# Weights by hardware queues with casts on chip, and a constant row summed earlier, in an eight-core attention kernel

## The reference

```
xn  = layernorm(x)                          # over the 1024 features
Q,K,V = xn@W1+b1, xn@W2+b2, xn@W3+b3        # each 1024 x 1024
attn  = softmax(Q K^T / 32)                 # 4096 x 4096 for each batch
out1  = (attn V) @ W4 + b4
W_real, W_imag = unfold(G1_R,G2_R), unfold(G1_I,G2_I)   # 512 x 512 each
out2  = [xr@Wr^T - xi@Wi^T + br,  xr@Wi^T + xi@Wr^T + bi] # complex linear layer on xn's halves
result = x + out1 + out2
```

## Time and profile before

| | us |
|---|---|
| median of 3 runs | 1297.14 |
| range of the runs | 1293.47 to 1345.95 |
| the profiled execution | 1296.3 |
| its span on the slowest core (core 6) | 1294.7 |
| spans of the 8 cores | 1287.4 to 1294.7 |
| PE busy | 1276.1 (99% of the span) |
| DVE, ACT, POOL busy | 522.5, 329.4, 169.5 |

### The profile page before, as it was taken

How to read it: one execution, slowest core, us unless ns; L and a number is a source line. 1 busy time by engine, 2 the same in 40 slices (tenths; PEclk the granted TensorE clock), 3 DMA queues, 4 the chain that set the end, 5 groups by cost and what they waited for, 6 DMA issues and landing times.

```text
span 1294.7 us, 16471 instructions; the slowest of 8 cores (1287.4 to 1294.7 us)
## 1 busy us (share of the span) xinstructions
PE 1276.1 (99%) x6142; PEld 588.7 (45%) x6142; DVE 522.5 (40%) x860; ACT 329.4 (25%) x463; POOL 169.5 (13%) x123
## 2 busy tenths in 40 slices
PE   6999998999999999999999999999999999999998
PEld 3555443444444444444444444444444444444444
DVE  4455661444144424442344333333433244414442
ACT  2453332312321122222112321122222212221111
POOL 2232132111011111111111111111111011101110
PEclk8999999999999999999999999999999999999999
DMA  9879294122222213321223223220233122322222
GB/s 134 202 188 203 49 196 73 33 66 66 65 65 65 66 33 82 76 71 33 66 65 79 52 52 79 66 66 33 65 79 80 39 65 66 65 65 66 65 66 66
DMA packets 178846, 100.74 MB, mean 78 GB/s; under 512 B 160824, under 2 KB 162896, under 8 KB 178768
## 3 DMA queue, kind: packets, MB, share of 16 engines
q1 hardware_dynamic: 173152, 91.28, 29.5%
q0 software_dynamic: 5408, 8.39, 4.4%
q10 hardware_dynamic: 208, 0.02, 0.0%
HBM read 51.43 MB, written 16.78 MB: 53 GB/s over the span
## 4 chain that ended last, share of the span: by engine, by line
PE 97%; DMA 2%; issue 0%; DVE 0%; POOL 0%; SPq 0%; ACT 0%; POOLq 0%; DVEq 0%; ACTq 0%
PE ring L788 34%; PE po L830 33%; PE ring L672 8%; PE pf L652 4%; PE po L652 4%; PE pf L815 2%; PE pf L801 2%; PE pf L808 2%; PE po L709 1%; PE ring L639 1%; PE pf L760 1%; PE po L760 1%; PE pf L709 1%; DMA V<-W 1%; DMA GT<-bim 1%; PE po L861 1%
## 5 line engine op out<-in xcount | busy, mean ns | idle before, releaser
L788 PE MATMUL ring<-XT,GT 128*128 128x512 bf16 x2048 | 447.4, 379 | 0.2 <-ACT Et L611 0.2
L830 PE MATMUL po<-V,ET 128*128 128x512 bf16 x1984 | 438.3, 379 | 0.0
L788 PEld LDWEIGHTS ring<-XT,GT 128*128 128x128 bf16 x2048 | 200.3, 98 | 242.0 <-issue 0.6
L830 PEld LDWEIGHTS po<-V,ET 128*128 128x128 bf16 x1984 | 194.1, 98 | 234.1
L475 DVE TENSOR_REDUCE mx<-ring 128x1 f32<-128x512 f32 x256 | 176.8, 691 | 210.8 <-PE ring L788 210.6
L501 DVE SCALAR_TENSOR_TENSOR xr<-po,rrv,xr 128x1024 f32<-128x1024 f32 x31 | 39.8, 1284 | 419.8 <-PE po L830 419.8
L326 POOL TENSOR_TENSOR xr<-xr,cb 128x1024 f32<-128x1024 f32 x32 | 75.0, 2343 | 939.6 <-DVE junk L480 939.6
L606 ACT ACTIVATE S<-ring 128x512 f32<-128x512 f32 x128 | 76.4, 597 | 423.7 <-DVE mx L475 423.6
L611 ACT ACTIVATE Et<-ring,ngm 128x2048 bf16<-128x2048 f32 x32 | 63.0, 1968 | 300.4 <-DVE ngm L494 300.4
L672 PE MATMUL ring<-XT,A 128*128 128x512 bf16 x512 | 113.7, 383 | 3.3 <-ACT GT L550 3.3
L672 PEld LDWEIGHTS ring<-XT,A 128*128 128x128 bf16 x512 | 50.4, 99 | 65.2 <-issue 5.9
(11 more groups left out here) (104 smaller groups left out, 641.8 us busy)
## 6 DMA issues: line engine op xcount, KB each, us to landing
xr<-x SPq DMA_DIRECT2D x40, 512.0 KB, 3.3
out<-xr SPq DMA_DIRECT2D x31, 512.0 KB, 2.6
S<-x SPq DMA_DIRECT2D x16, 512.0 KB, 6.1
Et<-x SPq DMA_DIRECT2D x8, 512.0 KB, 5.8
V<-W POOLq DMA_DIRECT2D x2, 1024.0 KB, 16.6
V<-W POOLq DMA_DIRECT2D x8, 256.0 KB, 18.4
V<-W POOLq DMA_DIRECT2D x4, 512.0 KB, 20.0
A<-W POOLq DMA_DIRECT2D x4, 512.0 KB, 8.9
```

Source lines behind the costliest of these rows:

```text
L788: mm = e.matmul(bank[tb % 4], GT[:, c, rows(i % 4)], XT[:, c, tb * 512:(tb + 1) * 512], start=(c == 0), stop=(c == 7))
L830: mm = e.matmul(po[:, v * 512:(v + 1) * 512], ET[:, i % 2, tj, :], V[:, tj, v * 512:(v + 1) * 512], start=(tj == 16), stop=(tj == 15))
```

## The change

- W4's left half no longer comes by one casting load of POOL. ACT issues four plain fp32 loads (pairs of row blocks p = 0 to 3) into a part of XT that is still unused (`W4stage`); DVE casts pairs 0 and 2, ACT pairs 1 and 3.
- W3's row 0 comes as fp32 by SP's first load (`W3stage`) and is cast by DVE. SP's small loads stand behind it, ACT's small loads have moved to SP.
- PE turns W3's row 0 before the G1 transposes, and row 1 inside fold piece 0, whose matmuls wait pair by pair.
- b4 is loaded on SP behind tile 18, the FFN biases behind tile 27, both into `xr[:, 1, :]`; DVE sums them behind tiles 24 and 28. ACT's `evict_g(0)` waits for the last weight operation (`s_wdv` 28) instead of the sums.
- PE's waits for the transposes of tiles 30 and 31 move from `g_group(0)` to the last block of the first scores.

The core of the diff:

```diff
-    bias_in = GT[:, 0:4, :].rearrange("p a n -> p (a n)").bitcast(F32)
+    bias_in = xr[:, 1, :]
+    W4stage = XT[:, :, 1024:2048].bitcast(F32)
+    W3stage = XT[:, 0:2, 2048:3072].bitcast(F32)
...
     def sync_program(e):
+        e.dma_start(W3stage, w3_d[rows(0), :].rearrange("p (c n) -> p c n", c=2)
+                    ).then_inc(d_w3[0], 16)
         for ri, g1 in enumerate((g1r_d, g1i_d)):
...
+        for ri, g2 in enumerate((g2r_d, g2i_d)):
+            e.dma_start(g2n[ri], bass.AP(g2.tensor, 0, [[16, 64], [1, 16]])).then_inc(d_g2, 16)
+        for s, b_d in enumerate((b1_d, b2_d, b3_d)):
+            e.dma_start(bn8[8 * s:8 * s + 8, :], bass.AP(b_d.tensor, 0, [[128, 8], [1, 128]])
+                        ).then_inc(d_bc, 16)
         e.wait_ge(d_w3[4], 16)
...
-        e.dma_start(b4_in, bass.AP(b4_d.tensor, 0, [[0, 128], [1, 1024]])).then_inc(d_bb, 16)
-        e.wait_ge(s_wdv, 28)
-        e.dma_start(bias_in[:, 0:512], ...
-        e.dma_start(bias_in[:, 512:1024], ...
+            if k == 18:
+                e.dma_start(b4_in, bass.AP(b4_d.tensor, 0, [[0, 128], [1, 1024]])
+                            ).then_inc(d_bb, 16)
+            elif k == 27:
+                e.wait_ge(s_cbe, 1)
+                e.dma_start(bias_in[:, 0:512], ...
+                e.dma_start(bias_in[:, 512:1024], ...
...
     def gpsimd_program(e):
-        load_w4(0)
...
-        for m in range(4):
+        for m in range(1, 4):
             load_row(m)
-        load_w4(1)
+        e.dma_start(W4half[1], w4_d[:, 512:1024].rearrange("(c p) n -> p c n", p=128)
+                    ).then_inc(d_w4b, 16)
...
     # vector_program
+        e.wait_ge(d_w3[0], 16)
+        e.tensor_copy(W3raw[:, 0, :].rearrange("p (c n) -> p c n", c=2), W3stage
+                      ).then_inc(s_vcast, 1)
+        for p in (0, 2):
+            e.wait_ge(d_w4a[p], 16)
+            e.tensor_copy(W4half[0][:, 2 * p:2 * p + 2, :], W4stage[:, 2 * p:2 * p + 2, :]
+                          ).then_inc(s_vcast, 1)
+            if p == 0:
+                evict_group(("w3", 0))
         e.wait_ge(s_gtp, 4)
...
-        evict_group(("w3", 0))
...
+            elif k == 24:
+                e.wait_ge(d_bb, 16)
+                e.wait_ge(s_w34e, 6)
+                e.tensor_add(cb[:, :], cb[:, :], b4_in).then_inc(s_cbe, 1)
+            elif k == 28:
+                e.wait_ge(d_bb, 48)
+                e.wait_ge(s_cbe, 1)
+                e.tensor_add(cb[:, :], cb[:, :], bias_in).then_inc(s_cbe, 1)
...
     # scalar_program, evict_g(0)
-                        e.wait_ge(s_cbe, 2)
+                        e.wait_ge(s_wdv, 28)
...
+        for p in range(4):
+            e.dma_start(W4stage[:, 2 * p:2 * p + 2, :],
+                        w4_d[256 * p:256 * (p + 1), 0:512].rearrange("(c p) n -> p c n", p=128)
+                        ).then_inc(d_w4a[p], 16)
+        e.wait_ge(d_g2, 32)
+        for ri in range(2):
+            e.activation(g2e[ri], ...
+        cast_w4(1)
+        cast_w4(3)
         for ri in range(2):
             e.wait_ge(s_gtp, ri + 1)
...
     # tensor_program, g_group(0)
-                    e.wait_ge(*turned(NT - 2))
-                    e.wait_ge(*turned(NT - 1))
...
+        turn(("w3", 0))
         e.wait_ge(s_idf, 1)
...
                 for j in range(8):
+                    if n == 0 and j in (0, 4):
+                        e.wait_ge(s_vcast, 2 + j // 4)
+                    elif n == 0 and j in (2, 6):
+                        if j == 6:
+                            turn(("w3", 1))
+                        e.wait_ge(s_acast, 1 + j // 4)
...
-        turn(("w3", 0))
-        turn(("w3", 1))
         fold34(0, 1)
...
         def scores(i, blocks):
             for tb in blocks:
+                if i == 0 and tb == NTB - 1:
+                    e.wait_ge(*turned(NT - 2))
+                    e.wait_ge(*turned(NT - 1))
```

More of the change, by code:

```diff
@@ L152, in build_nc @@
     s_pt = [sem("pt0"), sem("pt1")]
+    s_vcast = sem("vcast")
     s_idf, s_g1e, s_rep, s_cbe = sem("idf"), sem("g1e"), sem("rep"), sem("cbe")
@@ L161, in build_nc @@
     s_rr, s_cmb = sem("rr"), sem("cmb")
+    s_acast = sem("acast")
     s_g2e, s_g1x, s_g2x = sem("g2e"), sem("g1x"), sem("g2x")
@@ L174, in build_nc @@
     d_w1 = [sem(f"d_w1{k}") for k in range(4)]
-    d_w4 = [sem("d_w4a"), sem("d_w4b")]
+    d_w4a = [sem(f"d_w4a{p}") for p in range(4)]
+    d_w4b = sem("d_w4b")
     d_w3 = [sem(f"d_w3{k}") for k in range(8)]
@@ L224, in sync_program @@
                                           ).then_inc(d_w1t, 16)
-        e.dma_start(b4_in, bass.AP(b4_d.tensor, 0, [[0, 128], [1, 1024]])).then_inc(d_bb, 16)
-        e.wait_ge(s_wdv, 28)
[L227 to L230, removed]
+            if k == 18:
[3 more added lines that the diff above has]
+                e.wait_ge(s_cbe, 1)
+                e.dma_start(bias_in[:, 0:512], bass.AP(br_d.tensor, 0, [[0, 128], [1, 512]])
+                            ).then_inc(d_bb, 16)
+                e.dma_start(bias_in[:, 512:1024], bass.AP(bi_d.tensor, 0, [[0, 128], [1, 512]])
+                            ).then_inc(d_bb, 16)
         e.wait_ge(s_lnap, NT)
@@ L261, in gpsimd_program @@
     def gpsimd_program(e):
-        def load_w4(h):
-            e.dma_start(W4half[h], w4_d[:, 512 * h:512 * (h + 1)]
-                        .rearrange("(c p) n -> p c n", p=128)).then_inc(d_w4[h], 16)
         def load_pair(dst, src, k, done):
@@ L559, in evict_w34, with cast_w4 @@
                              AF.Identity).then_inc(s_w34e, 1)
[L561 to L565, removed]
+        def cast_w4(p):
+            e.wait_ge(d_w4a[p], 16)
+            e.activation(W4half[0][:, 2 * p:2 * p + 2, :], W4stage[:, 2 * p:2 * p + 2, :],
+                         AF.Identity).then_inc(s_acast, 1)
+        for p in range(4):
[4 more added lines that the diff above has]
+        for ri in range(2):
+            e.activation(g2e[ri], g2n[ri].unsqueeze(1).broadcast_to([64, 8, 16]),
+                         AF.Identity).then_inc(s_g2e, 1)
+        cast_w4(1)
+        cast_w4(3)
         for ri in range(2):
@@ L569, in scalar_program @@
                          AF.Identity).then_inc(s_g1x, 1)
[L570 to L573, removed]
         evict_group(("w3", 1))
@@ L633, in turn @@
                                   "w1": (d_w1[n // 2], W1raw, s_w1tp)}[kind]
-                e.wait_ge(d_w, 16)
+                if g == ("w3", 0):
+                    e.wait_ge(s_vcast, 1)
+                else:
+                    e.wait_ge(d_w, 16)
                 src = raw[:, n, :]
@@ L697, in fold34 @@
                 m, h = fold[n]
-                e.wait_ge(d_w4[h], 16)
+                if h == 1:
+                    e.wait_ge(d_w4b, 16)
                 if m < 8:
```

## The result

The changed kernel takes **1296.19 us** at the median of 20 runs (lowest 1294.85) beside 1294.09 of 20 runs of the kernel before. The ratio is **1.0018, 95% interval [1.0011, 1.0024]**: slower, by 2 us, where 7 us of gain were forecast. Executions in which one die was disturbed (up to 1454 us, 1498 for the kernel before) stand in these medians but are left out of all ratios and means here.

What follows compares the result with a forecast made beforehand. PE, busy 99% of the span, was taken as the bound, so only idle and slow-clock time could be won: 4.3 + 3.0 - 0.2 = 7.1 us from 1296.3 gives 1289.2, stated as 1289.5; range 1284 to 1295.5.

Steps and rivals of the forecast that it cites:

- T0: Start of PE's first work, the turn of W3's row 0: forecast at 8.9 us, bounds 8.0 and 10.1.
- in the middle 7.5: G1's landing behind row 0 on SP's queue: 7.5 us, between 6.6 alone and 8.3 with ACT sharing equally.
- the 8.3: Start: G1's landing behind row 0 if ACT's queue takes an equal share; a later landing would prove the forecast wrong.
- 7.9 of work and 2.4 of slow clock: PE's time from its first turn to the second fold piece: 7.9 us at full clock plus 2.4 for half clock.
- the 3.75 for the G1 transposes: PE's G1 transposes at the start, counted as 3.75 us at full clock within the 7.9 us of work.
- -3.0: Start: second fold piece at 19.2 instead of 22.21 us, 3.0 us earlier; bounds 1.1 and 4.2.
- The tail's mechanism: Behind the tiles: taking the bias wait out of ACT's path ends PE's stop in `g_group(0)`, winning 4.3 us.
- The moved loads: b4 and biases ahead of transposes on SP's queue: cost PE 0 to 0.5 us, 0.2 in the sum.
- The engines, not the queues, bound the start: Rival, start: three queues only divide the same bytes; gain only 0.5 to 1.5 us, 1291 to 1292; chance 0.22.
- The start gains more: Rival, start: clock up from the start and W4's pieces early, 6.3 us instead of 3.0, 1286; chance 0.12.

Runs made afterwards that it cites:

- e7: Changed kernel with two further, unread loads of G1 (32 KB) ahead of the real ones; ratio to the kernel before 1.0051.
- e5: Changed kernel with POOL waiting after W3's row 1 until W4's third piece has landed; ratio to the kernel before 1.0004.
- e3: Changed kernel with the two G1 loads ahead of W3's row 0 on SP's queue; ratio to the kernel before 1.0045.
- e4: Changed kernel with G1 ahead of W3's row 0 on SP's queue and in PE's order; ratio to the kernel before 1.0041.
- e2: Changed kernel with the constant row's part undone, so only the start is new; ratio to the kernel before 1.0032.
- e8: The kernel before, unchanged, run and profiled again; ratio 1.0000.
- e1: Kernel before with only the constant row's part (moved bias loads, sums and waits); ratio to the kernel before 0.9997.
- e9: Kernel before with only the constant row's part, run and profiled a second time; ratio to the kernel before 0.9998.
- e12: As e6, but POOL's hold ends at W4's pair 1 instead of pair 2; 1291.69 us, ratio to the kernel before 0.9984.
- e6: Changed kernel, loads by need: ACT issues row 0 (4 KB packets), then W4; SP small loads; POOL held; PE takes G1 first; ratio to the kernel before 0.9989.
- e11: The whole change, run again; ratio to the kernel before 1.0027.

## Why the prediction was wrong

*The step that failed* is T0: "in the middle 7.5" for G1's landing. It let an **equal share of bytes** go to ACT's queue and none to POOL's, and it left G1's own cost at what it had been on nearly empty queues, 3.4 us. Measured: row 0 landed at 1.06 + 9.2 = 10.3, already later than the 8.3 that was the bound for G1 behind it; G1 landed at 1.81 + 11.4 = 13.2 and 2.45 + 13.4 = 15.9, and T0 was 17.11 (14.5 on the earliest core, 15.8 in the mean) for 8.9, bounds 8.0 to 10.1. The last load of G1 is thus 5.6 us behind row 0. e7 and the packet counts show why: the share is one of packets, and G1 has 256 of them. e5 shows that POOL's part counts. How much of row 0's own lateness is turns, and how much the late beginning of SP's queue, stays open.

*Why it ended slower and not even.* Row 0's turn began hardly later than before: 15.8 for 15.5 in the mean over the cores. But before, the G1 transposes, the biases and G2 were done by then, in time in which PE had to wait anyway; now they stand behind it, 17.91 to 22.30 on core 4. e3 and e4 show that the G1 transposes in front are not enough: with G1 ahead on SP the turn comes at 17.6 and 17.7 in the mean, and e4, which has the transposes in front of it, begins the second piece at 27.2 where e3 begins it at 26.9. On its core 0 PE waits 1.66 us for the biases and 0.75 for G2 behind the turn, and six matmuls of the first piece take 2.74 us, half clock, as on all its cores.

*From T0 on the sum held, in part by luck.* It had 7.9 of work and 2.4 of slow clock, 10.3 us, to the second fold piece; measured 26.69 - 17.11 = 9.58. But the 3.75 for the G1 transposes, taken as full clock, was half clock: core 4's begin 0.21 us apart, as before's did, and 0.11 apart at their end, so 16 of them at full clock are about 1.8 us (16 x 0.11, an estimate). Against that too dear term stood waits that the sum did not have: 0.39 for G2, 0.37 for a cast and 1.06 for the eviction of row 1. The order of PE's work was as told, DVE's cast took 0.69 for 0.84, ACT's 1.04 for 1.02, and PE did not wait for W4's right half. The start came out at +3.2 (e2) for -3.0.

*The tail's mechanism was right, its size was not.* 4.3 us was the stop of the slowest core in one execution. Over the eight cores of that execution the same wait was 1.6, 1.2, 0, 0, 0, 0.3, 3.3 and 3.0, a mean of 1.2; in e8's 0.5. The median of the slowest core won 0.2 (e1) and 0.7 (e9).

*The moved loads cost nothing*, as said: b4 landed after 5.8 us and the last bias after 7.1, transposes after 6.9 at most on core 4 and 8.4 on the worst core, below the 9 that was forecast. POOL waited 12.8 us in all for transposes (4.7 to 11.6 on the cores of before), and PE for none on any of e1's or e9's cores.

*The rivals.* "The engines, not the queues, bound the start" was the nearest, and its argument was sound: the DMA share read 0.90 and 1.08, and more bytes early brought nothing. But it still counted 0.5 to 1.5 of gain, as it thought of row 0 among other pieces and not of small loads among large ones. The Trainium skill ("DMA: Bandwidth & Descriptors", "Issuing engines are not separate DMA queues") has it that several issuers save only issue time. Here that advice was right and too mild: e2 against e12 shows that the same bytes over the same three queues cost 3.2 us or win 1.5, by their order and the hold on POOL (with row 0 in larger packets, PE's order changed, and some 0.3 us of the constant row in e12). "The start gains more" rested on a clock of 1.00 at 4 to 8 us; that reading was no evidence, see below. No case of the prediction ended slower through the start, so its range had no room for the result: T0 and its bound of 10.1 were built from before's landings, when POOL's queue alone had large loads.

## What to carry to other kernels

When loads are spread over queues, count packets, not bytes: a queue gets turns, a load of many small rows costs as many turns as a large one, and loads that no one needs yet take turns from the one that the critical engine waits for. Put what is needed first at the head of every queue, and hold the rest back until just before it is due, no longer (e6 and e12 differ only in this). A wait of the slowest core in one profiled execution is not worth its own length: 3.3 us here, 1.2 and 0.5 in the mean over the cores of two executions, and 0.2 and 0.7 us of the slowest core's median when it was gone.

## What the runs showed of the hardware beyond that

- **The clock's record can mislead, the durations don't.** In the window 16 to 24 us e6's core 4 reads a clock of 1.00 and e12's core 0 reads 0.69 (the columns before it are busy times), and in both the six matmuls of the first piece take 2.74 us, against 1.47 in the changed kernel:

```profile
16.00:24.00 8.00, 7.69 (x45) 4.10 (x45) 5.06 (x8) 4.51 (x8) 5.31 (x10) 1.00 0.76 98
```

```profile
16.00:24.00 8.00, 8.00 (x46) 4.47 (x46) 5.06 (x8) 4.36 (x8) 3.57 (x7) 0.69 1.05 137
```

  The trace of e6's core 4 holds no record of the clock before 19.9 us, nor that of the changed kernel's core 4 before 20.2, and the view counts time without a record as 1.00. For core 6 of the kernel before the first record is at 8.4, so the 1.00 at 4 to 8 us was no measurement. Likewise the first turn of the changed kernel, after 17 us of rest, took 1.01 us under a reading of 1.00, where a turn takes 0.61 later. The sixteen G1 transposes that were priced at 3.75 as full speed took 3.11 there, the later ones at twice the pace of the first; 3.75 was not full speed.
- **A late start mostly has a cheaper clock.** In the changed kernel PE comes to the first fold piece with hardly a pause, and on all eight cores of its profile the first six matmuls take 1.47 us. Over it and its variants with the same order on PE (e11, e2, e3, e5, e7) that holds for 39 of 48 cores; the other 9 take 2.74. The earlier, interrupted starts of e4, e6 and e12 take 2.55 to 2.74 on all 24. That is one reason why e12 is only 4 to 6 us faster than the changed kernel though PE's first instruction is 9 us earlier: 1.27 us on these six matmuls. Its waits for the biases and G2 are another.
